# A graph attention layer with a bit-decoding MLP on one core: spins ahead of the last two tiles' features, edges prepared on Pool, x tiles loaded behind operand 6, and the MLP's second bias as a hidden unit

## The chip, the core and the metric

The kernel runs on one core of a Trainium2 chip. The metric is the device time of one execution in microseconds (us). The engines are TensorE (PE in the profile), VectorE (DVE), ScalarE (ACT), GpSimd (POOL) and SyncE (SP). SP, Pool and, where told to, ScalarE issue DMA transfers, each from a queue of its own.

## What is computed

There are N = 1250 nodes with 512 features, 20000 edges sorted by destination, and H = 4 heads of 512 columns. `_layernorm` has no scale. Cut to what matters:

```
xn    = layernorm(x)
q,k,v = xn @ Wq + bq, xn @ Wk + bk, xn @ Wv + bv          # each (n, 4, 512)
alpha = sum(q[dst] * k[src]) / sqrt(512);  attn = softmax of alpha over the edges of one dst
agg   = segment_sum(attn * v[src], dst)                    # (n, 4 * 512)
xa    = agg + xn @ Wskip + bskip
x     = x + gamma * layernorm(xa @ Wlin + blin + xa[:, :512]) + beta
z     = layernorm(x)
# three MLPs (and, or, xor): only inputs 0, 1, 44, 45, 46 can be nonzero and only output 64 is used
nibbles = argmax(z[:, 16:32] > .5), ... (four of them);  flags = z[:, 1:4]
sel   = the chosen MLP's  relu(feat @ w1 + b1) @ w2[:, 64] + b2[64], for rows 0 and 1
out   = z with 2 * one_hot(clip(round(sel), 0, 15)) added at columns 80:96 and 96:112 where active
x     = x + out
```

## The kernel before, in words

**Splits.** Each fp32 matrix is split into a high and a low part (fp32r), and a product is three matmuls of 512 columns (`mm3`, L1533 to L1535): high by high, high by low, low by high.

**Weight products.** Per head, the weights are multiplied first: G = Wq by Wk, M = Wv by Wlin, K = Wskip by Wlin, numbered p = 0 to 11. A job ("P", p, i) is the row block i (of KC = 4) of product p. Operand n (`opnd[n % 4]`) is the n-th weight in the order Wq, Wk, Wv, Wlin, Wskip of each head. SP loads it into `stage[n % 2]`, except operands 2 and 3 (Wv and Wlin of head 0), which go to `early[0]` and `early[1]`; ScalarE writes its high part (`split_hi`, L771; for the early ones `split_hi_halves`, L833, in two column halves), VectorE its low part (`split_lo`, L1012; `split_lo_halves`, L1020). Before Wlin of head 0 is split, VectorE adds the identity to its diagonal. A finished block goes from PSUM to `prod_parts` in two parts, high by ScalarE (L808) and low by VectorE (L1075), and Pool's queue stores it to HBM (`store_product`, L624). `prod_parts` has room for one product, so the high part of block i of the next product waits on `prod_out[i]`, the landing of that store.

**Edges.** In between, TensorE counts edges: for each tile of 128 destination nodes it multiplies one-hot rows of the edges' destinations and sources (`count_part`, L1652, bf16, 105 columns), by quarters of the edge tiles, behind jobs of products 1 to 10. VectorE builds the one-hot rows (`onehots`, L1034 and L1043) one job ahead. For this `edge_places` (L1079) turns the edge numbers into places and weights; it runs on VectorE at p = 0, i = 2.

**x.** Ten tiles of 128 rows. Tiles 0 to 3 go to `x_aside`, tiles 4 to 9 to `acc`. VectorE measures them (`x_moments`) at p = 2 and 3, at the jobs in MEASURED; x_moments(0) waits for all three loads. They are normalized and transposed between later jobs.

**Heads.** Each of four heads runs ten destination tiles d: scores (L1533 to L1535 into ps_s), mask, exp, weighing by counts, a transposition through HBM (`regroup` on SP's queue), and `outputs`, 10 x 3 matmuls of 512 columns. The first three heads are a loop, the last one is written out (`last_head`).

**The end.** In the last head each finished tile goes through add_out (L1347), ScalarE's squares (L908, L915), `centre` (L1377), `residual` (L1384), Pool's inverse spread (`inverse_spread`, L660 and L662), the features (VectorE L1393 to L1407, Pool's `choice` L684 to L688 and `choose` L1417), a transposition (`turn_features`, L1781), a copy by ScalarE (L929), two hidden matmuls (`hidden`, L1791, 3 x 160 columns), two dot products with w2 on VectorE (`dots`, L1431) and `results`. The second bias is chosen on Pool (`chosen_bias`, L693 and L694) and added in `results`. All but columns 80 to 112 of tiles 8 and 9 is stored ahead (`store_rest`); these columns (`store_result`, L568) follow, tile 9 from VectorE first, then tile 8 from Pool, both on SP's queue. At the program's start TensorE runs 18 matmuls on `ones` (`spin`, L1661), which nothing reads.

Of the kernel before, what the change touches and what calls it, by code (L numbers as in the profile page):

```python
# [33 lines left out]
N = 1250  # L34
# [29 lines left out]
HID = 160  # L64
SPINS = 18
BY_POOL = NT - 2
# [97 lines left out]
def graph_layer(nc, x, src, dst, weights, bias_cols, blin, gamma, beta, mlp_w1, mlp_w2, mlp_b2, out):  # L164
# [3 lines left out]
    with ExitStack() as ctx:  # L168
# [130 lines left out]
        b2_bc = put("b2_bc", [P, OPS], F32)  # L299
# [30 lines left out]
        s_b2 = [small[0:R, 80 + i:81 + i] for i in range(2)]  # L330
        s_act, s_flag = [small[0:R, 82:83], flag_pool[0:R, 0:1]], [small[0:R, 83:86], flag_pool[0:R, 1:4]]
        s_part = small[0:R, 86:89]
# [3 lines left out]
        x_in, edges_in, bias_in, tail_in = sem("x_in"), sem("edges_in"), sem("bias_in"), sem("tail_in")  # L336
        blin_in = sem("blin_in")
# [81 lines left out]

        def half_cols(i):  # L420

            return slice(D // 2 * i, D // 2 * i + D // 2)
# [63 lines left out]
        def _(sp):  # L486
# [60 lines left out]
            sp.dma_start(b2_bc[0:R, :], mlp_b2.partition_broadcast(R)).then_inc(tail_in, 16)  # L547
# [12 lines left out]

            def store_result(t):
                rows = min(R, N - R * t)
                some = slice(LO_HI_OUT, LO_HI_OUT + 32)
                if t == BY_POOL:
                    sp.wait_ge(o_pool, 1)
                else:
                    sp.wait_ge(o_ready, t)
                sp.dma_start(out[R * t:R * t + rows, some], acc[0:rows, t, some]).then_inc(out_done, 16)  # L568
# [25 lines left out]
            for t in (NT - 1, NT - 2):  # L594
                store_result(t)
# [1328 lines left out]
```

## Time and profile before

| | |
|---|---|
| three runs | 1003.58, 1234.95 and 1005.67 us; median 1005.67 |
| profiled execution | 1004.65 us; span from first to last instruction 1002.5 us |
| mean granted TensorE clock | 0.993 |
| busy share of the span | PE 98%, PEld (weight load) 80%, DVE 58%, ACT 33%, POOL 11% |
| DMA | 115.84 MB, mean 116 GB/s; in the first of 40 slices 327 GB/s |
| chain that ended last | PE 94%, DVE 2%, DMA 2%, ACT 1%, issue 1% |

All times in rows count from the span's start. A matmul's record overlaps the next one's, so the distance from start to start tells its cost, and "idle before" is shown only where the engine stood. The granted clock is a share of full speed (1.00 is 2.4 GHz, 0.50 is 1.2 GHz).

### The profile page before, as it was taken

The page shows a single profiled execution, that of the slowest core. Times are in us where ns is not written, and L with a number is a line of the kernel's source. Part 1 is how long each engine was busy: PE and PEld are TensorE (multiplying, and loading weights), DVE is VectorE, ACT ScalarE, POOL GpSimd, SP SyncE. Part 2 cuts the span into 40 slices and gives each one's busy share as a digit, 9 for nine tenths or more (in the row PEclk, how much of TensorE's full clock was granted, in tenths as well). Part 3 has the DMA queues.
Part 4 walks back from the last instruction along what each step waited for, and adds up shares of the span by engine and source line. Part 5 has one row for each costly group of instructions (what it writes and reads, how often), then busy time and mean ns, then how long its engine had stood idle before and what let it go on. Part 6 is the DMA issues. An engine that isn't in the chain of part 4 may idle for free.

```text
span 1002.5 us, 13135 instructions
## 1 busy us (share of the span) xinstructions
PE 984.4 (98%) x4841; PEld 804.8 (80%) x4841; DVE 579.2 (58%) x1225; ACT 335.0 (33%) x531; POOL 107.7 (11%) x232
## 2 busy tenths in 40 slices
PE   9999999999999999999999999999999999999994
PEld 6667777688888888888888888888888888888883
DVE  6899996452445446226454542354464325788786
ACT  4446554102233223114222321233232213435342
POOL 2121101000000000000000000000000000345465
PEclk9999999999999999999999999999999999999997
DMA  9856554400152344005323420161334103443421
GB/s 327 286 210 210 218 192 189 168 2 1 53 189 68 91 122 146 28 1 157 111 79 105 159 83 1 27 215 53 105 80 163 52 1 83 154 121 105 143 83 40
DMA packets 43561, 115.84 MB, mean 116 GB/s; under 512 B 5472, under 2 KB 26044, under 8 KB 40172
## 3 DMA queue, kind: packets, MB, share of 16 engines
q1 hardware_dynamic: 38892, 98.21, 31.5%
q0 software_dynamic: 4608, 16.78, 4.3%
q8 instruction: 43, 0.70, 0.3%
q14 instruction: 18, 0.15, 0.0%
HBM read 70.07 MB, written 44.90 MB: 115 GB/s over the span
## 4 chain that ended last, share of the span: by engine, by line
PE 94%; DVE 2%; DMA 2%; ACT 1%; issue 1%; SPq 0%; DVEq 0%
PE ps_o L1533 10%; PE ps_o L1534 9%; PE ps_o L1535 9%; PE ps_s L1534 9%; PE ps_r L1533 9%; PE ps_s L1535 9%; PE ps_s L1533 9%; PE ps_r L1535 9%; PE ps_r L1534 9%; PE ps_t L1533 2%; PE ps_t L1535 2%; PE ps_t L1534 2%; DMA stage<-in_Wk 1%; PE ps_s L1612 1%; PE ps_s L1652 1%; DMA early<-in_Wlin 1%
## 5 line engine op out<-in xcount | busy, mean ns | idle before, releaser
L1534 PE MATMUL ps_s<-xT_lo,tT 128*128 128x512 f32 (+1 forms) x480 | 168.7, 351 | 0.0
L1535 PE MATMUL ps_s<-xT_hi,tT 128*128 128x512 f32 (+1 forms) x480 | 168.4, 351 | 0.0
L1533 PE MATMUL ps_s<-xT_hi,tT 128*128 128x512 f32 (+1 forms) x480 | 168.1, 350 | 0.0
L1533 PE MATMUL ps_o<-y,pT 128*128 128x512 f32 x380 | 148.6, 391 | 0.0
L1534 PE MATMUL ps_o<-y,pT 128*128 128x512 f32 x380 | 148.0, 389 | 0.0
L1535 PE MATMUL ps_o<-y,pT 128*128 128x512 f32 x380 | 148.0, 389 | 0.0
L897 ACT ACTIVATE prob<-prob,nbias 128x1250 f32<-128x1250 f32 x40 | 53.7, 1342 | 269.5 <-DVE nbias L1296 269.5
L1290 DVE CUSTOM_DVE_ANT_0 prob<-ps_s,maskb 128x1250 f32<-128x1250 f32 x40 | 58.2, 1456 | 128.9 <-issue 128.9
L1534 PEld LDWEIGHTS ps_s<-xT_lo,tT 128*128 128x128 f32 x480 | 90.7, 189 | 14.1
L1533 PEld LDWEIGHTS ps_s<-xT_hi,tT 128*128 128x128 f32 x480 | 90.5, 189 | 14.0
L1535 PEld LDWEIGHTS ps_s<-xT_hi,tT 128*128 128x128 f32 x480 | 90.8, 189 | 12.5
L880 ACT ACTIVATE pT<-whole 128x640 fp32r<-128x640 f32 x78 | 57.1, 737 | 103.3 <-PE ps_o L1535 97.8
L1303 DVE CUSTOM_DVE_ANT_0 prob<-prob,count 128x1250 f32<-128x1250 f32 x40 | 58.4, 1459 | 46.5 <-ACT prob L897 46.5
L1535 PEld LDWEIGHTS ps_o<-y,pT 128*128 128x128 f32 x380 | 71.3, 188 | 14.9
L1533 PEld LDWEIGHTS ps_o<-y,pT 128*128 128x128 f32 x380 | 71.5, 188 | 14.4
L1534 PEld LDWEIGHTS ps_o<-y,pT 128*128 128x128 f32 x380 | 71.4, 188 | 13.7
L651 POOL MEMSET row_mask<- 108x1 f32 x1 | 0.1, 99 | 688.3 <-DMA w_raw<-in_mlp_w 688.3
L1347 DVE SCALAR_TENSOR_TENSOR acc<-ps_o,zinv,acc 128x512 f32<-128x512 f32 x38 | 28.4, 748 | 78.9 <-PE ps_o L1535 78.0
L1533 PE MATMUL ps_r<-xT_hi,gbuf 128*128 128x512 f32 (+1 forms) x192 | 67.4, 351 | 0.0
L1534 PE MATMUL ps_r<-xT_lo,gbuf 128*128 128x512 f32 (+1 forms) x192 | 67.4, 351 | 0.0
L1535 PE MATMUL ps_r<-xT_hi,gbuf 128*128 128x512 f32 (+1 forms) x192 | 67.4, 351 | 0.0
L1270 DVE TENSOR_TENSOR y<-ps_r,y 128x512 fp32r<-128x512 f32 x40 | 27.4, 684 | 66.4 <-ACT y L867 66.4
(293 smaller groups left out, 1763.0 us busy)
## 6 DMA issues: line engine op xcount, KB each, us to landing
regrouped<-prob SPq DMA_DIRECT2D x156, 160.0 KB, 2.8
whole<-regrouped SPq DMA_DIRECT2D x39, 640.0 KB, 3.9
products<-prod_parts POOLq DMA_DIRECT2D x32, 512.0 KB, 3.9
gbuf<-products SPq DMA_DIRECT2D x4, 2048.0 KB, 8.2
mbuf<-products SPq DMA_DIRECT2D x4, 2048.0 KB, 9.0
stage<-in_Wskip SPq DMA_DIRECT2D x4, 1024.0 KB, 6.0
stage<-in_Wq SPq DMA_DIRECT2D x3, 1024.0 KB, 5.5
stage<-in_Wk SPq DMA_DIRECT2D x3, 1024.0 KB, 5.9
```

The costliest lines, as they stand in the source:

```text
L651: link(nc.gpsimd.memset(row_mask[:, 0:1], 1.0))
L880: nc.scalar.activation(pT[:, 0, a:b, :].rearrange("p k (q b) -> p k q b", q=Q), whole[:, :, a:b, :].rearrange("p q k b -> p k q b"), ACT.C ...
L897: nc.scalar.activation(at_prob, at_prob, ACT.Exp, scale=SCALE, bias=nbias[0:R, d:d + 1]).then_inc(exp_done, 1)
L1270: nc.vector.tensor_tensor(y[:, 1, a, :], ps_r[:, local % 2, :], y[:, 0, a, :].bitcast(F32), ALU.subtract).then_inc(rot_free, 1)
L1290: nc.vector.tensor_tensor_reduce(at_prob, ps_s[0:R, 0:N], maskb[0:R, :], 1.0, -0.1 * MASKED, ALU.subtract, ALU.max, top[0:R, d:d + 1]).the ...
L1303: nc.vector.tensor_tensor_reduce(at_prob, at_prob, count[0:R, d, 0:N], 1.0, 0.0, ALU.mult, ALU.add, zsum[0:R, d:d + 1]).then_inc(prob_read ...
L1347: nc.vector.scalar_tensor_tensor(out=acc[0:R, d, :], in0=out_bank(d, last)[0:R, :], scalar=zinv[0:R, d:d + 1], in1=acc[0:R, d, :], op0=ALU ...
L1533: nc.tensor.matmul(out_, a[0], b[0], start=start, stop=False)
L1534: nc.tensor.matmul(out_, a[0], b[1], start=False, stop=False)
L1535: return nc.tensor.matmul(out_, a[1], b[0], start=False, stop=stop)
L1612: ins = nc.tensor.matmul(ps_uv[:, a, :], bpad[:, 1 - a, at:at + 2 * H], w[s][:, k, :], start=(h == 0 and k == 0 and s == 0), stop=(h == H ...
L1652: nc.tensor.matmul(ps_s[0:R, 0:NP], onehot_dst[t % RING][0:ER, a:a + R], onehot_src[slot][0:ER, j, 0:NP], start=(t == window(d)[0]), stop= ...
```

## The change

It has five parts.

1. HID grows from 160 to 162. The new hidden unit 160 has weight 1 at the constant feature, so its value is 1 for the chosen MLP, and its entry in w2 is b2[64]; unit 161 is zero. The load of b2, Pool's `chosen_bias` and its operand in `results` go.
2. `edge_places` moves from VectorE to Pool, ahead of all product stores; the last step is two instructions there. VectorE waits for `edges_ready` where the work stood. The four edge loads move ahead of Wv's. VectorE's half split (2, 0) moves ahead of the first product's saves.
3. The loads of x tiles 4 to 8 and of tile 9 move behind the load of operand 6. The wait for three blocks' stores ahead of them goes. x_moments(0) waits for tiles 0 to 3 only, x_moments(4) for the others.
4. In the last head the low columns of tile 8 (L1393) become a step of their own, `low_columns`, and the residual of tile 9 comes between them and the rest of tile 8's features. Tile 8's result is stored from ScalarE's queue.
5. TensorE runs 40 spins on the identity (read as bf16, 256 columns each) ahead of tile 8's feature transposition, and 8 ahead of tile 9's.

```diff
-HID = 160
+HID = 162
+LAST_SPINS = (40, 8)
...
-            for n in (3, 2):
-                sp.dma_start(early[n - 2][:], weights[n][0]).then_inc(early_in[n - 2], 16)
+            sp.dma_start(early[1][:], weights[3][0]).then_inc(early_in[1], 16)
             for i, ends in enumerate((src, dst)):
                 for a, w in EDGE_ROWS:
                     sp.dma_start(edge_i[a:a + w, i, :], ends[a:a + w, :]).then_inc(edges_in, 16)
+            sp.dma_start(early[0][:], weights[2][0]).then_inc(early_in[0], 16)
...
-            for i in range(KC - 1):
-                sp.wait_ge(prod_out[i], 16)
-            sp.dma_start(acc[:, X_ASIDE:NT - 1, :], x_tiles[:, X_ASIDE:NT - 1, :]).then_inc(x_in, 16)
-            sp.wait_ge(pads_ready, 1)
-            sp.dma_start(acc[0:LAST_ROWS, NT - 1, :], x[full:N, :]).then_inc(x_in, 16)
             for n in load_order():
                 sp.wait_ge(split_ready[n % 2], n // 2 - 1)
                 sp.dma_start(stage[n % 2][:], weights[n % 5][n // 5]).then_inc(stage_in[n % 2], 16)
+                if n == 6:
+                    sp.dma_start(acc[:, X_ASIDE:NT - 1, :], x_tiles[:, X_ASIDE:NT - 1, :]).then_inc(x_more_in, 16)
+                    sp.wait_ge(pads_ready, 1)
+                    sp.dma_start(acc[0:LAST_ROWS, NT - 1, :], x[full:N, :]).then_inc(x_more_in, 16)
...
-            for t in (NT - 1, NT - 2):
-                store_result(t)
+            sp.wait_ge(o_ready, NT - 1)
+            sp.dma_start(out[full:N, result_cols], acc[0:LAST_ROWS, NT - 1, result_cols]).then_inc(out_done, 16)
...
+            def edge_places():
+
+                pool.wait_ge(edges_in, 32 * len(EDGE_ROWS))
+                link(nc.gpsimd.tensor_copy(edge_f[0:ER], edge_i[0:ER]))
+                source, place = edge_f[0:ER, 0, :], at_plane[0:ER, :]
+                link(nc.gpsimd.tensor_scalar(place, source, -float(NP // 2), 1.0 / NP, ALU.add, ALU.mult))
+                link(nc.gpsimd.tensor_scalar(place, place, ROUND, None, ALU.add))
+                link(nc.gpsimd.tensor_scalar(place, place, ROUND, None, ALU.subtract))
+                nc.gpsimd.tensor_scalar(weight_i[0:ER, :], place, DIGIT * 2.0 ** 23, ONE_BITS, ALU.mult, ALU.add)
+                link(nc.gpsimd.tensor_scalar(place, place, -float(NP), None, ALU.mult))
+                nc.gpsimd.tensor_tensor(edge_place[0:ER, :], place, source, ALU.add).then_inc(edges_ready, 1)
+
+            edge_places()
             for p in range(3 * H):
...
-                link(nc.gpsimd.tensor_scalar(sel_, sel_, s_b2[t % 2], 0.0, ALU.add, ALU.max))
-                link(nc.gpsimd.tensor_scalar(sel_, sel_, 15.0, ROUND, ALU.min, ALU.add))
+                link(nc.gpsimd.tensor_scalar(sel_, sel_, 0.0, 15.0, ALU.max, ALU.min))
+                link(nc.gpsimd.tensor_scalar(sel_, sel_, ROUND, None, ALU.add))
...
             choice(NT - 2)
-            chosen_bias(NT - 2)
             z_factors(NT - 1)
             choice(NT - 1)
-            chosen_gate(NT - 2)
+            gates(NT - 2)
             gates(NT - 1)
             results(NT - 2)
...
                 feat_copy(NT - 1)
+                act.wait_ge(o_pool, 1)
+                act.dma_start(out[R * BY_POOL:R * BY_POOL + R, result_cols],
+                              acc[0:R, BY_POOL, result_cols]).then_inc(out_done, 16)
...
-            split_lo_halves(3)
+            split_lo_half(3, 0)
+            split_lo_half(3, 1)
+            split_lo_half(2, 0)
             for job in JOBS:
...
                 if p == 0:
                     if i == 0:
-                        split_lo_halves(2)
+                        split_lo_half(2, 1)
                     if i == 2:
-                        edge_places()
+                        dve.wait_ge(edges_ready, 1)
...
                 centre(NT - 1)
+                low_columns(NT - 2)
+                residual(NT - 1)
                 features(NT - 2)
-                residual(NT - 1)
                 choose(NT - 2)
...
-            def spin():
-
-                some = ones[:].bitcast(BF16)
-                pe.wait_ge(pool_step, 1)
-                for _ in range(SPINS):
+            def spin(some, times):
+
+                for _ in range(times):
                     nc.tensor.matmul(ps_s[:, 0:2 * P], some[:, 0:P], some, start=True, stop=True)
...
-                for t in range(NT - 2, NT):
+                for t, times in ((NT - 2, LAST_SPINS[0]), (NT - 1, LAST_SPINS[1])):
+                    spin(ident[:].bitcast(BF16), times)
                     turn_features(t)
                     hidden(t)
```

## Rows read from the trace of the kernel before

**Rows 1.** Windows: stretch, length, busy of each engine, clock, DMA share, GB/s.
```profile
110.00:985.00 875.00, 875.00 (x4293) 727.34 (x4291) 471.56 (x955) 273.99 (x413) 76.41 (x159) 1.00 0.32 100
985.00:1002.50 17.50, 4.84 (x14) 2.50 (x12) 10.37 (x41) 3.90 (x11) 10.44 (x35) 0.63 0.13 41
```

**Rows 2.** Timeline of TensorE: start, duration, instruction, idle before and its releaser.
```profile
32.40 0.41 PE L1652 MATMUL ps_s<-onehot_src,onehot_dst 125*128 125x105 bf16 x5
34.55 1.25 PE L1652 MATMUL ps_s<-onehot_src,onehot_dst 125*128 125x105 bf16 x5 [1.74 <-DVE onehot_dst L1043]
...
50.74 0.99 PE L1652 MATMUL ps_s<-onehot_src,onehot_dst 125*128 125x105 bf16 x4 [0.95 <-DVE onehot_dst L1043]
...
79.89 1.05 PE L1652 MATMUL ps_s<-onehot_src,onehot_dst 125*128 125x105 bf16 x6
```

**Rows 3.** Timeline of VectorE in the start.
```profile
15.25 2.36 DVE L1020 TENSOR_TENSOR opnd_lo<-early,opnd_hi 128x1024 fp32r<-128x1024 f32 x2
18.77 0.69 DVE L1075 TENSOR_TENSOR prod_parts<-ps_t,prod_parts 128x512 fp32r<-128x512 f32 x1 [1.16 <-ACT prod_parts L808]
...
22.84 0.32 DVE L1083 CAST edge_f<-edge_i 125x320 f32<-125x320 int32 x1
...
24.68 0.60 DVE L1034 TENSOR_TENSOR onehot_src<-node_id,edge_place 125x420 bf16<-125x420 f16 x1
...
28.41 0.68 DVE L1075 TENSOR_TENSOR prod_parts<-ps_t,prod_parts 128x512 fp32r<-128x512 f32 x1
...
34.16 1.37 DVE L1043 TENSOR_SCALAR onehot_dst<-node_id,edge_f,edge_p 125x256 bf16<-125x256 f16 x5
...
47.03 2.29 DVE L1012 TENSOR_TENSOR opnd_lo<-stage,opnd_hi 128x2048 fp32r<-128x2048 f32 x1 [2.80 <-ACT opnd_hi L771]
```

**Rows 4.** Timeline of ScalarE in the start.
```profile
26.03 0.60 ACT L808 ACTIVATE prod_parts<-ps_t 128x512 fp32r<-128x512 f32 x1 [5.90 <-DMA products<-prod_parts]
...
45.09 1.92 ACT L771 ACTIVATE opnd_hi<-stage 128x2048 fp32r<-128x2048 f32 x1 [5.79 <-DMA stage<-in_Wk]
```

**Rows 5.** Timeline of SP's queue: the issue of operand 6.
```profile
33.65 0.34 SPq L509 DMA_DIRECT2D stage<-in_Wk  x1
```

**Rows 6.** Timelines of Pool and VectorE; last, a group of Pool's by form.
```profile
19.77 0.92 POOL L624 DMA_DIRECT2D products<-prod_parts  x1 [15.56 <-DVE prod_parts L1075]
...
73.74 2.27 DVE L1012 TENSOR_TENSOR opnd_lo<-stage,opnd_hi 128x2048 fp32r<-128x2048 f32 x1
...
74.59 1.99 POOL L638 TENSOR_TENSOR nmr<-mv,rstd 128x10 f32<-128x10 f32 x1
76.67 0.34 POOL L639 TENSOR_SCALAR nmr<-nmr 128x10 f32<-128x10 f32 x1
...
L730 POOL TENSOR_TENSOR xres<-xres,beta_bc 128x512 f32<-128x512 f32 x9 | 11.7, 1295 | 0.9 <-DMA xres<-in_x 0.9
```

**Rows 7.** Timeline of the end, all engines.
```profile
988.77 0.95 POOL L662 TENSOR_TENSOR rstd<-veps,eps_pow 128x1 f32<-128x1 f32 x1
989.33 0.32 DVE L1393 TENSOR_SCALAR z_low<-acc,mv,rstd 128x80 f32<-128x80 f32 x1
...
990.75 0.76 DVE L1384 SCALAR_TENSOR_TENSOR acc<-centred,rstd,xres_last 128x512 f32<-128x512 f32 x1
...
995.26 0.66 DVE L1431 SCALAR_TENSOR_TENSOR ps_t<-ps_t,w_bc 128x480 f32<-128x480 f32 x1
...
996.29 1.14 PE L1791 MATMUL ps_t<-w_parts,featT 108*128 108x480 f32 x2 [0.41 <-ACT featT L929]
...
999.70 0.74 SPq L568 DMA_DIRECT2D out<-acc  x2
```

**Rows 8.** Windows of the end, columns as in rows 1.
```profile
985.00:990.00 5.00, 1.70 (x8) 1.08 (x6) 3.52 (x13) 1.18 (x5) 2.67 (x7) 0.94 0.14 52
...
989.00:989.50 0.50, 0.00 (x0) 0.00 (x0) 0.46 (x2) 0.00 (x0) 0.50 (x1) 0.93 0.00 0
```

**Rows 9.** The spins at the start: ns min/median/max, first and last start.
```profile
L1661 PE MATMUL ps_s<-ones x18: 394/421/421, 2.3 to 5.9; 128*128 128x256 bf16 x18
```

More of the change, by code:

```diff
@@ L329, in graph_layer @@
         s_gate = [small[0:R, 78 + i:79 + i] for i in range(2)]
-        s_b2 = [small[0:R, 80 + i:81 + i] for i in range(2)]
         s_act, s_flag = [small[0:R, 82:83], flag_pool[0:R, 0:1]], [small[0:R, 83:86], flag_pool[0:R, 1:4]]
-        s_part = small[0:R, 86:89]
         s_sel, hot = [small[0:R, 90 + 2 * i:92 + 2 * i] for i in range(2)], small[0:R, 96:128]
-        x_in, edges_in, bias_in, tail_in = sem("x_in"), sem("edges_in"), sem("bias_in"), sem("tail_in")
-        blin_in = sem("blin_in")
+        x_in, edges_in, edges_ready, bias_in, tail_in = sem("x_in"), sem("edges_in"), sem("edges_ready"), sem("bias_in"), sem("tail_in")
+        blin_in, x_more_in = sem("blin_in"), sem("x_more_in")
         g_in, m_in, xres_in, out_done = sem("g_in"), sem("m_in"), [sem(f"xres_in{i}") for i in range(3)], sem("out_done")
@@ L559, in store_rest @@
                     sp.dma_start(out[R * t:R * t + rows, a:b], acc[0:rows, t, a:b]).then_inc(out_done, 16)
[L561 to L568, printed above, removed]
             def store(t):
@@ L1013, in split_lo, with split_lo_half @@
                                                 ALU.subtract).then_inc(split_ready[odd], 1)
-            def split_lo_halves(n):
-                for half, high in enumerate((half_hi[n - 2], hi_ready[n % 2])):
-                    some = half_cols(half)
-                    dve.wait_ge(high, 1)
-                    ins = nc.vector.tensor_tensor(opnd[n][1][:, :, some], raw(n)[:, :, some],
-                                                  opnd[n][0][:, :, some].bitcast(F32), ALU.subtract)
-                    if half:
-                        ins.then_inc(split_ready[n % 2], 1)
-                    elif n == 2:
-                        ins.then_inc(half_split, 1)
+            def split_lo_half(n, half):
+                some = half_cols(half)
+                dve.wait_ge(hi_ready[n % 2] if half else half_hi[n - 2], 1)
+                ins = nc.vector.tensor_tensor(opnd[n][1][:, :, some], raw(n)[:, :, some],
+                                              opnd[n][0][:, :, some].bitcast(F32), ALU.subtract)
+                if half:
+                    ins.then_inc(split_ready[n % 2], 1)
+                elif n == 2:
+                    ins.then_inc(half_split, 1)
             def onehots(b):
@@ L1386, in residual, with low_columns @@
                                                accum_out=stats[0:R, t, 2:3]).then_inc(res_ready, 1)
-            def features(t):
+            def low_columns(t):
                 z = z_low[t % 2]
@@ L1394, in features @@
                                         ALU.subtract, ALU.mult).then_inc(z_low_ready, 1)
+            def features(t):
+                z = z_low[t % 2]
                 dve.wait_ge(z_low_ready, t + 1)
@@ L1439, in results @@
                 dve.wait_ge(gate_ready, t + 1)
-                chain(nc.vector.tensor_scalar(sel_, sel_, s_b2[t % 2], 0.0, ALU.add, ALU.max))
-                chain(nc.vector.tensor_scalar(sel_, sel_, 15.0, ROUND, ALU.min, ALU.add))
+                chain(nc.vector.tensor_scalar(sel_, sel_, 0.0, 15.0, ALU.max, ALU.min))
+                chain(nc.vector.tensor_scalar(sel_, sel_, ROUND, None, ALU.add))
                 for r in range(2):
@@ L1654, in count_part @@
                                      stop=(t == window(d)[-1])).then_inc(onehot_used, 1)
-            def spin():
-                some = ones[:].bitcast(BF16)
-                pe.wait_ge(pool_step, 1)
-                for _ in range(SPINS):
+            def spin(some, times):
+                for _ in range(times):
                     nc.tensor.matmul(ps_s[:, 0:2 * P], some[:, 0:P], some, start=True, stop=True)
-            spin()
+            pe.wait_ge(pool_step, 1)
+            spin(ones[:].bitcast(BF16), SPINS)
             first_product()
@@ L1894 @@
         for r in range(2):
[L1895 to L1897 removed]
+            feats[:, o, r:4:2, r, o, 0:HID - 2] = np.stack([w1[o][i] for i in (0, 1)])
+            feats[:, o, 4 + 3 * r:7 + 3 * r, r, o, 0:HID - 2] = np.stack([w1[o][i] for i in (46, 44, 45)])
+            feats[:, o, 10 + r, r, o, 0:HID - 2] = b1[o]
+            feats[:, o, 10 + r, r, o, HID - 2] = 1.0
     arrays = {
```

43 lines of the change are left out of this document (12 added, 31 removed).

## The prediction, made before the change was run

> **What bounds the kernel now.** I read the windows by stretch first: from 110 to 985 us TensorE's busy time equals the stretch, and the last 17.5 us hold only 4.84 us of it, at a mean granted clock of 0.63 [rows 1]. No edit shortens TensorE's work in the full stretch, so time is won or lost in two places: the start, up to about 100 us, and the end, after the last wide matmul. Busy times of matmuls overlap, so in the start I went by TensorE's timeline and looked for small matmuls with a releaser or a stretched duration. There are three stalls, each in the matmuls that count edges [rows 2]. The first, at 34.55: idle 1.74 us, and then five matmuls take 1.25 us where five took 0.41 just before; 1.74 + 0.84 = 2.6 us. The second, at 50.74: idle 0.95 us, and four take 0.99 instead of 0.41 x 4/5 = 0.33; 1.6 us. The third, at 79.89: six take 1.05 instead of 0.49; 0.6 us. The releaser of the first two is VectorE's one-hot rows (L1043), so VectorE's timeline comes next, then what VectorE waited for.
>
> **The start, first stall.** VectorE works without a gap from 22.84 us to 34.16 + 1.37 = 35.5 us, the end of the one-hots that TensorE waits for. First in it stands the edge preparation, from 22.84 to 24.68: 1.84 us, which moves to Pool [rows 3]. The half split of operand 2 that moves ahead of the first product's save also fills the 1.16 us in which VectorE waited before 18.77 [rows 3]. So the first one-hots could start up to 1.84 + 1.16 = 3.0 us earlier, less some 0.6 us, my guess for Wv landing behind four edge transfers: 22.3 us, if Pool is done. That gain isn't passed on whole. ScalarE starts the high part of product (1,0) at 26.03 us, when the store of product (0,0) has landed, and takes 0.60 [rows 4]; so VectorE's save of (1,0), at 28.41 before [rows 3], can't start ahead of 26.7. From that save to the one-hots' end are 35.5 - 28.4 = 7.1 us of gapless work, which gives 33.8: a gain of 1.7, or 1.9 if the store lands a little earlier.
>
> That store stands on Pool's queue, issued at 19.77 us [rows 6], and the edge work is now ahead of it there. The edges follow Wlin, which has landed when VectorE splits it at 15.25 [rows 3]; say 14 us. The trace has no Pool row of 125x160: below it lies 128x10 with one input, 0.34 us, above it 128x512 with two, 1.29 us [rows 6]. That is 0.34 and 1.9 ns an element, so at most 0.64 for 160 columns and 0.95 for the copy of 320. Eight instructions: 2.7 to 5.4 us; I take 4, in the middle as the shapes are, done near 18 us if nothing holds Pool.
>
> Something can hold it. A Pool instruction of 128x10 with two inputs took 1.99 us, begun at 74.59 while VectorE ran a split of two SBUF inputs from 73.74 to 76.01, and ended after that split [rows 6]. The splits of operands 3 and 2 run from 15.25 on, 1.18 us a half [rows 3], just where Pool's edge chain falls.
> The Trainium skill, SBUF — State Buffer, section "Who interferes with whom", says that a VectorE instruction with two SBUF inputs contends with a GpSimd instruction that reads SBUF, and that whichever issues second blocks fully. The row of 1.99 us agrees. By that rule the forecast of a free Pool is too good; the held case below is what it would make of this kernel.
> Priced from rows, if four half splits hold one Pool instruction each for about 1 us, the chain ends near 22. The store leaves 2 us or so later than 19.77; it took 6.3 us before, behind loads that will have drained further, so I let it land near 27. VectorE then reaches the end of the one-hots at 27.0 + 0.6 + 7.1 = 34.7, a gain of 0.8. Between 1.7 (free) and 0.8 (held), with ends 1.9 and 0, I take **1.1**.
>
> **The start, second stall.** VectorE sat idle 2.80 us ahead of the split of operand 6 at 47.03 [rows 3], since ScalarE waited 5.79 us for Wk until 45.09 [rows 4]. Wk was issued at 33.65 [rows 5], behind the x tiles, and took 11.4 us to land. Now the x tiles go behind it. Issued at about 32.7, Wk needs to be in place when ScalarE is through with its saves and VectorE with its own work, 2.8 + 1.1 us ahead of 45.09: by 41.2, after 8.5 us. The store of the same congested start took 6.3 with half the bytes [rows 4, 6], so this isn't sure. If it is in time, VectorE gains 1.1 + 2.8 = 3.9 us by this point and TensorE needs 1.1 + 1.6 = 2.7, a margin of 1.2: the whole **1.6** goes (1.0 if Wk lands 1.8 us late, 0 if it lands no earlier). Load 7 leaves SP some 0.9 us later than it would (two x issues); its split comes seven microseconds behind operand 6's, which covers it, as it covers x itself, whose tiles from 4 on are first read there. The wait for the zeroed pad rows, now on SP ahead of load 7, is over since the program's start.
>
> **Later stalls.** VectorE comes out 1.2 us further ahead of TensorE than before, and the third stall of 0.6 can go, with another like it near 96; from 0 to 1.1, I take **0.5**. The start gives 1.1 + 1.6 + 0.5 = **3.2**, ends 0 and 4.6.
>
> **The end.** Of the window from 985 to 990 us TensorE fills the first 1.70, so its last wide matmul ends at 986.7, and the clock goes to 0.50 only in the last tenth of a microsecond ahead of 989.5 (0.93 over that half microsecond) [rows 8]. Then VectorE, ScalarE and Pool pass the last tile's statistics around. VectorE writes the low columns of tile 8 at 989.33, goes through its features until 990.75 and only then runs the residual of tile 9 [rows 7]. Now the residual comes right behind the low columns, once Pool's spread is ready: 988.77 + 0.95 = 989.72, or 989.8. That is 0.95 us earlier, and what hangs on it (square, spread, features and choice of tile 9) moves along up to the dot products of tile 8, from 995.26 to 994.3 [rows 7]. The features of tile 8 are 0.25 later, about 992, which still leaves 2.3 us for their transposition, copy and hidden matmuls.
> VectorE then has four dot products of 0.66 us: 994.3 + 2.65 = 997.0. Before, the last two waited for tile 9's hidden matmuls, begun at 996.29, a pair of which took 1.14 us at clock 0.50 [rows 7, 8]; the first was done at about 997.05, and two dot products later it was 998.4. So the gain is 1.4 if the hidden matmuls are in time, and 0.95 if the clock stays at half.
> The spins: 18 of 256 columns at the start lie (5.9 - 2.3)/17 = 0.21 us apart [rows 9]; at full clock eight matmuls of 512 columns pass in 1.70 us [rows 8], 0.21 each, so 256 take 0.11. Forty behind 986.7 take 4.3 us, until 991.0, a microsecond ahead of the transposition; eight behind tile 8's hidden matmuls take 0.9, until about 994, ahead of tile 9 as well. They delay nothing then. The bias leaves Pool's chain, off the path, and six columns more in a dot product (486 for 480) add 0.66/80 = 0.01 us. Both results end near 998.2, and their stores, 0.74 us for two issues in a row on one queue [rows 7], leave from two: 0.37 more. ScalarE's queue is used for the first time, which no row prices; -0.6 to +0.2 around it. The end gives 1.4 + 0.4 = **1.8**, ends 0.7 and 2.2.
>
> **Sum.** The profiled execution took 1004.65 us, 2.15 beside its span, and lies 1.0 under the median of 1005.67. 1004.65 - 3.2 - 1.8 = **999.7 us**.
>
> **Rivals.** (1) The splits hold Pool's chain so long that the first stall and the later ones stay: 1004.65 - 1.6 - 1.8 = 1001.3. For it: the 1.99 us row; against: only four splits, with saves between them. (2) Wk still lands late, since the product stores share the transfers: 1004.65 - 1.6 - 1.8 = 1001.3 too, by the first stall and the later ones alone. (3) The clock falls under the spins near 989.4: twenty-four are through, sixteen at 0.21 end near 992.8, the eight follow late hidden matmuls by 1.7 us, and tile 9's transposition comes some 1.4 us later than before. With 0.4 won by the stores: 1004.65 - 3.2 + 1.0 = 1002.5. Against it: the clock stood through 2.7 us without any matmul. (4) The other side: Pool gets no turn until VectorE itself stops for it near 22.8, and needs 3.5 us more. The store leaves at 26.3 and with the old 6.3 us lands at 32.6; VectorE's save starts at 33.2, 4.8 us behind before, and TensorE with it. Against it stand the second stall and the end, 3.4: 1004.65 + 4.8 - 3.4 = 1006.1. It decides from a landing at 31.2 on (28.4 - 0.6 + 3.4).
>
> **Chances.** Forecast, with its own range 998 to 1001: 0.55. Rival 1: 0.17, rival 2: 0.13, rival 3: 0.09, rival 4: 0.06. The range goes from 997.0, nearly the high ends of both sums (4.6 and 2.2 give 997.9) and 0.9 of scatter, to 1004.0, rivals 1 to 3 and 1.5 of scatter; it leaves rival 4 out. A measurement tells about 2%, 20 us, from no change. No case reaches that either way, as all the idle time of start and end sums to less: 0.02 faster, 0.96 within, 0.02 slower for what I haven't seen.
>
> **What would show it.** First stall: VectorE's first one-hots before 23.5 us and under 1.9 us lost near 33; Pool instructions of over 1 us in the edge chain would show the hold. Second: ScalarE's high part of operand 6 begun by 41 us. The end: a residual of tile 9 some 3.1 us behind the last wide matmul, not 4.05; a clock of 1.00 up to the last hidden matmul; and transpositions that don't follow right on a spin. The prediction fails if the store of product (0,0) lands past 28 us, if the spins run at 0.21, or if the shifts in the start meet a wait for a transfer that was hidden before.

## The result, and the profile after

The changed kernel takes 998.47 us (median of six runs, 998.14 to 1000.15) where the kernel before takes 1004.23 (six runs, median). The ratio is 0.9947, with an interval from 0.9933 to 0.9961: 5.3 us faster, between 3.9 and 6.7, which is within 2%. The ratio compares fast executions alone and leaves out one of the kernel before, which took 1234.95 us. The profiled execution took 998.3 us, its span 996.4. The forecast was 999.7 and the range 997.0 to 1004.0.

I divide each execution at the end of the last wide matmul of the last tile (L1522 to L1524), which is 982.24 us here and was 986.70 before. What lies behind it, the end part, takes 996.4 - 982.24 = 14.16 us; before it took 15.8. So the two profiled executions differ by 4.46 us in the start and by 1.64 in the end part.

**The start.** TensorE's timeline has the same groups of counting matmuls as [rows 2]:

```profile
30.20 0.41 PE L1641 MATMUL ps_s<-onehot_src,onehot_dst 125*128 125x105 bf16 x5
33.27 0.98 PE L1641 MATMUL ps_s<-onehot_src,onehot_dst 125*128 125x105 bf16 x10
...
47.96 0.46 PE L1641 MATMUL ps_s<-onehot_src,onehot_dst 125*128 125x105 bf16 x6
```

TensorE waits ahead of none of them. The ten at 33.27 are the two groups that stood at 32.40 and 34.55 before; they take 0.98 us for 0.82, so 0.2 is left of the first stall's 2.6. At 47.96 stand six in one group; before they were two, a wait, and the four at 50.74. VectorE's timeline answers to [rows 3]:

```profile
16.32 3.75 DVE L1013 TENSOR_TENSOR opnd_lo<-early,opnd_hi 128x1024 fp32r<-128x1024 f32 x3
...
22.92 0.58 DVE L1027 TENSOR_TENSOR onehot_src<-node_id,edge_place 125x420 bf16<-125x420 f16 x1
...
26.86 0.69 DVE L1068 TENSOR_TENSOR prod_parts<-ps_t,prod_parts 128x512 fp32r<-128x512 f32 x1
...
32.61 1.36 DVE L1036 TENSOR_SCALAR onehot_dst<-node_id,edge_f,edge_p 125x256 bf16<-125x256 f16 x5
```

The three half splits run without a gap, the first one-hots start 1.76 us earlier than before, and the save of block (1,0), at 26.86 for 28.41, starts as soon as it can. From there to the end of the one-hots, 33.97, are 7.1 us, as forecast. ScalarE's timeline answers to [rows 4]:

```profile
26.15 0.60 ACT L799 ACTIVATE prod_parts<-ps_t 128x512 fp32r<-128x512 f32 x1 [5.01 <-DMA products<-prod_parts]
...
37.91 1.92 ACT L762 ACTIVATE opnd_hi<-stage 128x2048 fp32r<-128x2048 f32 x1 [0.18 <-DMA stage<-in_Wk]
```

The store of product (0,0) landed at 26.15, and operand 6 was there 7.2 us earlier than before. Pool's timeline is new here:

```profile
15.18 0.45 POOL L633 CAST edge_f<-edge_i 125x320 f32<-125x320 int32 x1 [10.97 <-DMA edge_i<-in_dst]
15.72 0.34 POOL L635 TENSOR_SCALAR edge_i<-edge_f 125x160 f32<-125x160 f32 x1
16.15 0.64 POOL L636 TENSOR_SCALAR edge_i<-edge_i 125x160 f32<-125x160 f32 x1
16.88 1.16 POOL L637 TENSOR_SCALAR edge_i<-edge_i 125x160 f32<-125x160 f32 x1
18.12 0.87 POOL L638 TENSOR_SCALAR edge_p<-edge_i 125x160 int32<-125x160 f32 x1
19.06 1.49 POOL L639 TENSOR_SCALAR edge_i<-edge_i 125x160 f32<-125x160 f32 x1
20.63 1.56 POOL L640 TENSOR_TENSOR edge_place<-edge_i,edge_f 125x160 f16<-125x160 f32 x1
22.14 2.38 POOL L613 DMA_DIRECT2D products<-prod_parts  x3
```

One form, 125x160 with one input, takes 0.34 us before VectorE's splits begin and up to 1.49 beside them (four of them, between 16.32 and 21.80): the hold of the prediction. In run e9 (below), whose chain comes later, the last instruction (L640) takes 0.52 us, as no split is left then, and not 1.56:

```profile
22.58 0.52 POOL L640 TENSOR_TENSOR edge_place<-edge_i,edge_f 125x160 f16<-125x160 f32 x1
```

The chain of seven takes 7.0 us, and the store leaves at 22.14, with two others behind it.

Two things more stand in TensorE's timelines. The later stalls are gone: before, the groups at 76.63, 79.89 [rows 2] and 96.31 took 0.2, 0.6 and 0.5 us more than an undisturbed one, 1.3 altogether, and after none does. And the first weight product starts 1.04 us later than before (7.05 us for 6.01), of which 0.87 is left at 33.27; in the other traces of kernels with this start it begins between 5.83 and 6.73, so this is scatter and no gain or loss of the change. The first line is of the kernel before, the others are of the changed one:

```profile
96.31 0.99 PE L1652 MATMUL ps_s<-onehot_src,onehot_dst 125*128 125x105 bf16 x6
...
7.05 0.73 PE L1564 MATMUL ps_t<-opnd_hi 128*128 128x512 f32 x2 [0.69 <-ACT opnd_hi L819]
...
76.30 0.47 PE L1641 MATMUL ps_s<-onehot_src,onehot_dst 125*128 125x105 bf16 x6
...
92.04 0.46 PE L1641 MATMUL ps_s<-onehot_src,onehot_dst 125*128 125x105 bf16 x6
```

**The end.** The windows of the end, columns as in [rows 1], and its timeline, which answers to [rows 7]:

```profile
982.24:987.00 4.76, 4.38 (x40) 3.69 (x38) 3.43 (x12) 2.62 (x7) 2.44 (x8) 1.00 0.15 57
987.00:992.00 5.00, 3.11 (x14) 1.63 (x14) 3.88 (x17) 1.37 (x4) 4.22 (x17) 1.00 0.27 85
992.00:996.40 4.40, 0.00 (x0) 0.00 (x0) 1.59 (x7) 0.00 (x0) 1.29 (x4) 0.67 0.04 7
```

```profile
985.30 0.75 DVE L1367 SCALAR_TENSOR_TENSOR acc<-centred,rstd,xres_last 128x512 f32<-128x512 f32 x1
...
987.00 0.19 POOL L662 TENSOR_SCALAR veps<-stats 128x1 f32<-128x1 f32 x1 [0.20 <-ACT junk L906]
...
989.83 0.66 DVE L1419 SCALAR_TENSOR_TENSOR ps_t<-ps_t,w_bc 128x486 f32<-128x486 f32 x1
...
990.72 1.00 PE L1779 MATMUL ps_t<-w_parts,featT 108*128 108x486 f32 x2 [0.41 <-ACT featT L920]
...
993.23 0.25 POOL L713 TENSOR_TENSOR acc<-acc,hot_pool 128x32 f32<-128x32 f32 x1
993.51 0.38 ACTq L984 DMA_DIRECT2D out<-acc  x1
993.54 0.19 DVE L1436 TENSOR_TENSOR acc<-acc,ones 128x32 f32<-128x32 f32 x1
993.76 0.32 SPq L584 DMA_DIRECT2D out<-acc  x1
```

The residual of tile 9 comes 3.06 us behind the last wide matmul and the first dot product 7.59; before it was 4.05 and 8.56. The granted clock is 1.00 as far as 992, behind the last hidden matmul; only then does it fall to its lower level (1.2 GHz). The second of the two result stores is issued at 993.76. What follows stands in no timeline, but in the view by source line, where the end of the program has line 169 (168 before), that of the block around it. Each engine's sequencer has a drain there, and SP's branch stands behind its wait for all stores:

```profile
L169 POOLq EVENT_SEMAPHORE  x2: 17/17/17, 996.2 to 996.3; - x2
...
L169 POOLq DRAIN  x1: 3005/3005/3005, 993.2 to 993.2; - x1
...
L169 SPq COMPARE_BRANCH  x1: 38/38/38, 995.1 to 995.1; - x1
L169 SPq DRAIN  x1: 7/7/7, 995.3 to 995.3; - x1
```

These columns are duration in ns (min, median, max) and first and last start in us. So SP is through at 995.1. Pool's drain starts with Pool's last instruction, takes 3.0 us, and ends at 996.2, 2.7 us behind that instruction's end; then the program ends. The kernel before has the same pair:

```profile
L168 POOLq DRAIN  x1: 3062/3062/3062, 999.2 to 999.2; - x1
...
L168 SPq COMPARE_BRANCH  x1: 38/38/38, 1001.5 to 1001.5; - x1
```

The expectations of the experiments were written without these rows, and argue with dot products and stores.

### The profile page after: what moved, and what is told of

It reads as the page before. It is cut to its first block, busy times and chain, and to the rows that moved or that the text cites. A ratio compares the mean times of both kernels' runs of the same rounds, so it can differ in the third digit from the quotient of the medians.

```text
span 996.4 us, 13209 instructions
## 1 busy us (share of the span) xinstructions
PE 986.7 (99%) x4889; PEld 807.9 (81%) x4889; DVE 576.6 (58%) x1219; ACT 335.9 (34%) x531; POOL 108.8 (11%) x219
## 4 chain that ended last, share of the span: by engine, by line
PE 99%; DMA 1%; DVE 0%; issue 0%; ACT 0%; SPq 0%
PE ps_o L1522 10%; PE ps_o L1523 10%; PE ps_o L1524 10%; PE ps_r L1522 9%; PE ps_r L1524 9%; PE ps_r L1523 9%; PE ps_s L1523 9%; PE ps_s L1524 9%; PE ps_s L1522 9%; PE ps_t L1522 3%; PE ps_t L1524 2%; PE ps_t L1523 2%; PE ps_s L1601 1%; PE ps_s L1641 1%; PE ps_t L1564 1%; PE ps_s L1648 1%
## 5 line engine op out<-in xcount | busy, mean ns | idle before, releaser
L1524 PE MATMUL ps_s<-xT_hi,tT 128*128 128x512 f32 (+1 forms) x480 | 168.4, 351 | 0.0
L1522 PE MATMUL ps_s<-xT_hi,tT 128*128 128x512 f32 (+1 forms) x480 | 168.1, 350 | 0.0
L1522 PE MATMUL ps_o<-y,pT 128*128 128x512 f32 x380 | 148.6, 391 | 0.0
L1524 PE MATMUL ps_o<-y,pT 128*128 128x512 f32 x380 | 148.0, 389 | 0.0
L1522 PEld LDWEIGHTS ps_s<-xT_hi,tT 128*128 128x128 f32 x480 | 90.6, 189 | 14.2 <-issue 0.2
L1524 PEld LDWEIGHTS ps_s<-xT_hi,tT 128*128 128x128 f32 x480 | 90.7, 189 | 12.5
L1524 PEld LDWEIGHTS ps_o<-y,pT 128*128 128x128 f32 x380 | 71.3, 188 | 14.9
L1522 PEld LDWEIGHTS ps_o<-y,pT 128*128 128x128 f32 x380 | 71.4, 188 | 14.4
L1522 PE MATMUL ps_r<-xT_hi,gbuf 128*128 128x512 f32 (+1 forms) x192 | 67.4, 351 | 0.0
L1524 PE MATMUL ps_r<-xT_hi,gbuf 128*128 128x512 f32 (+1 forms) x192 | 67.4, 351 | 0.0
```

Of the source, the lines that this page charges most:

```text
L1522: nc.tensor.matmul(out_, a[0], b[0], start=start, stop=False)
L1524: return nc.tensor.matmul(out_, a[1], b[0], start=False, stop=stop)
```

## The experiments on the start

A ratio is a run's time over that of the kernel before in the same batch, with its 95% interval. The end part is the span less the end of the last wide matmul, in the profiled execution. All ratios below lie within 2% of 1.

**Run e5_before_again**: the kernel before once more, unchanged.

> The kernel before, unchanged, for the scatter of its start. Two kernels with the same start (the spins alone, the residual first) ended their last wide matmul at 983.9 and 984.3 us, not 986.7. Theory A (Wk's landing behind the x tiles varies between executions, and with it the second stall): the end of the last wide matmul lies between 983.5 and 987, and where it is early, ScalarE's wait for Wk ends near 42 and not 45 us. Theory B (the edits at the end moved the start by their code): it is at 986.7 again, within 0.3. The stretch behind it stays at 15.8 us under both.

One run: 1002.74 us. The last wide matmul ends at 984.91, 1.8 us earlier than in the profile of before. ScalarE's wait for Wk ends at 42.95, not 45.09, and there is no second stall; the first is there:

```profile
34.94 1.24 PE L1652 MATMUL ps_s<-onehot_src,onehot_dst 125*128 125x105 bf16 x5 [1.40 <-DVE onehot_dst L1043]
```

Two experiments below have the start of the kernel before as well: their last wide matmuls end at 984.28 (e3) and 983.91 (e4), and neither has the second stall. So the start scatters by 2.8 us between executions, and the 1.6 of the second stall was a draw of the profiled one: three of the four traces with this start lack it. The first stall scatters too: 2.6, 2.2 (e5), 1.8 (e3) and 1.6 us (e4).

**Run e1_edges_alone**: the kernel before with part 2 of the change only.

```diff
-            for n in (3, 2):
-                sp.dma_start(early[n - 2][:], weights[n][0]).then_inc(early_in[n - 2], 16)
+            sp.dma_start(early[1][:], weights[3][0]).then_inc(early_in[1], 16)
...
+            sp.dma_start(early[0][:], weights[2][0]).then_inc(early_in[0], 16)
...
-            split_lo_halves(3)
+            split_lo_half(3, 0)
+            split_lo_half(3, 1)
+            split_lo_half(2, 0)
...
-                        edge_places()
+                        dve.wait_ge(edges_ready, 1)
```

> The kernel before with the edges' preparation on Pool, their loads ahead of Wv's and the moved half split, nothing else. Theory A (the parts of the start depend on each other): the first stall of 2.6 us nearly goes, but Wk is still queued behind the x tiles, so VectorE's split of operand 6 stays near 47 us while TensorE comes 2.4 us earlier, and the second stall grows from 1.6 to 3 or 4 us. The last wide matmul ends 0 to 1 us ahead of 986.7; the time falls by 0 to 1 us. Theory B (each stall is worth its own length): the second stall stays at 1.6, the time falls by 2.4 us. Theory C (Pool, held by VectorE's splits, gives the stall back): the first one-hots start after 24 us, the store of product (0,0) lands past 28, no gain and a first stall of over 2 us.

Ratio 0.9999 (0.9988 to 1.0011), median 1003.38 beside 1003.82. TensorE's timeline:

```profile
33.36 1.07 PE L1652 MATMUL ps_s<-onehot_src,onehot_dst 125*128 125x105 bf16 x10
...
50.10 1.04 PE L1652 MATMUL ps_s<-onehot_src,onehot_dst 125*128 125x105 bf16 x4 [1.68 <-DVE onehot_dst L1055]
```

The first stall is gone, but 1.68 + 0.71 = 2.4 us are lost at the second place, where VectorE's work hangs on Wk, for which ScalarE waited until 44.45. Alone, this part only brings TensorE earlier to the next wait.

**Run e2_x_behind_operand6**: the kernel before with part 3 only.

```diff
-            for i in range(KC - 1):
-                sp.wait_ge(prod_out[i], 16)
-            sp.dma_start(acc[:, X_ASIDE:NT - 1, :], x_tiles[:, X_ASIDE:NT - 1, :]).then_inc(x_in, 16)
...
+                if n == 6:
+                    sp.dma_start(acc[:, X_ASIDE:NT - 1, :], x_tiles[:, X_ASIDE:NT - 1, :]).then_inc(x_more_in, 16)
...
```

> The kernel before with only the x tiles' loads moved behind operand 6. Theory A: VectorE's idle 2.8 us before the split of operand 6 goes, the second stall of 1.6 with it, and the later ones of 0.6 and 0.5 too; the first stays at 2.6. The last wide matmul ends 1.6 to 2.7 us earlier, the time falls by as much. Rival (the load was late for other transfers' sake, the product stores): ScalarE still waits for Wk past 43 us, the second stall stays above 1 us, and the time falls by under 1 us.

Ratio 0.9989 (0.998 to 0.9999), median 1002.43. Wk is in place at 39.58, where ScalarE waits 0.23 us for it. The first stall stays:

```profile
34.63 1.25 PE L1653 MATMUL ps_s<-onehot_src,onehot_dst 125*128 125x105 bf16 x5 [1.55 <-DVE onehot_dst L1042]
```

**Run e8_start_edits_both**: the diffs of e1 and e2 together on the kernel before, with its old end.

> The kernel before with both edits of the start (edges on Pool, x behind operand 6) and the old end. Theory A (they depend on each other): the first and second stalls both go, the last wide matmul ends at 982 to 982.5, 2 to 4 us earlier than before's executions, more than the sum of the two alone (0 and 1.1 us by the times). Theory B (they add): 1.1 us. The end stays at 15.8.

Ratio 0.9967 (0.9956 to 0.9979), median 1000.67: 3.3 us, where the parts gave 0.1 and 1.1. The last wide matmul ends at 982.19, as in the changed kernel, and the end part takes 15.8, as before. So most of the gain of the start belongs to the pair: two waits in a row on one path. Without the first alone TensorE stops at the second (e1); without the second alone it still stops at the first (e2). By the times this is only just clear of the noise: the two parts together reach up to 3.2 us at the ends of their intervals, and the pair lies between 2.1 and 4.4. The stalls in the three traces carry it.

**Run e9_edges_behind_wv**: the changed kernel with the edge loads behind Wv, as they were before.

```diff
             sp.dma_start(early[1][:], weights[3][0]).then_inc(early_in[1], 16)
+            sp.dma_start(early[0][:], weights[2][0]).then_inc(early_in[0], 16)
             for i, ends in enumerate((src, dst)):
                 for a, w in EDGE_ROWS:
                     sp.dma_start(edge_i[a:a + w, i, :], ends[a:a + w, :]).then_inc(edges_in, 16)
-            sp.dma_start(early[0][:], weights[2][0]).then_inc(early_in[0], 16)
```

> The changed kernel with the four edge loads behind Wv again, as before the change. In the five traces so far with the edge loads ahead of Wv, VectorE gets Wlin at 13.9 to 14.5 us, in the five without at 12.8 to 13.6. Theory A (that is lost on no path: TensorE's second product starts near 21.6 in both): the edges land some 2 us later, Pool's chain ends near 24 instead of 22, the store of product (0,0) lands at 27 to 28, and the time is 0.5 to 1.5 us longer. Theory B (the early landing of Wlin is worth its 0.9 us): the time falls by up to 0.9 us.

Ratio 0.9965 (0.9952 to 0.9978), median 998.86; run e10, in the same batch, has 0.995 and 998.72. The edges land 2.0 us later, at 17.21, and Pool ends its chain at 23.1. VectorE waits for it:

```profile
23.14 0.60 DVE L1027 TENSOR_TENSOR onehot_src<-node_id,edge_place 125x420 bf16<-125x420 f16 x1 [1.01 <-POOL edge_place L640]
```

TensorE's ten matmuls at 32.96 take 1.57 us, 0.6 more than after; but in e10, with the order of the change, they take 1.70. So the order of the loads is worth between 0.1 us (medians) and 1.5 (ratios), too little to tell.

**Run e11_edge_chain_longer**: the changed kernel with four Pool instructions more in the edge chain, which multiply by one.

```diff
+                for _ in range(4):
+                    link(nc.gpsimd.tensor_scalar(place, place, 1.0, None, ALU.mult))
```

> The changed kernel with four more instructions of 125x160 (times 1.0) in Pool's edge chain. The chain took 7.0 us. Theory A (Pool stands on the path through the store of product (0,0), as rival 4 had it): the chain ends 2.5 to 4 us later, near 25 to 26, VectorE waits for it from 22.9 on, the store lands at 28 to 30 and the first stall grows by 2 to 4 us, the time as much. Theory B (the store's landing is set by the transfers ahead of it, and VectorE has room): it still lands by 27, and the time grows by under 1.5 us.

Ratio 0.9977 (0.9967 to 0.9986), median 1001.2: 2.5 us slower than e10 in the same batch. The four take 4.59 us beside the splits, the chain ends at 23.87, and VectorE waits for it:

```profile
23.90 0.60 DVE L1029 TENSOR_TENSOR onehot_src<-node_id,edge_place 125x420 bf16<-125x420 f16 x1 [1.99 <-POOL edge_place L642]
```

The store of product (0,0) lands at 27.17, a microsecond later than after, and the first stall is back with 1.42 + 0.84 us at 34.02. VectorE's one-hots end at 34.99, a microsecond later than after. So Pool's chain stands on the path; after, it ended 0.7 us ahead of VectorE's use (22.2 to 22.92), but the store followed it at once. There is a second loss, in the windows, columns as in [rows 1]:

```profile
36.00:40.00 4.00, 4.00 (x12) 2.62 (x11) 4.00 (x12) 1.76 (x2) 1.26 (x2) 0.57 0.98 322
```

Behind the stall the clock falls to its lower level for nearly these four microseconds, and wide matmuls start every 0.43 us, not every 0.23. Run e7 has the same, by chance:

```profile
36.00:40.00 4.00, 4.00 (x12) 3.07 (x11) 4.00 (x13) 1.87 (x2) 1.38 (x2) 0.57 0.98 357
```

There the store landed at 27.68. From the stalled matmuls to the next group are 7.4 us (34.53 to 41.93); in e12, whose stall at 34.46 was 0.3 us shorter and whose clock stayed, 5.8. So a first stall can cost 1.6 us more than its own length, and 1.6 of the 2.2 us by which the last wide matmul ends later in e11 than after are of this kind. The stall of the kernel before [rows 2] was longer and left the clock at 1.00; what decides stays open. The two slowest executions of e9 (1001.84 and 1001.56 us, at a mean clock of 0.997 and 0.996, where the other five have 0.998 or 0.999 and at most 999.72) may be of this kind; they have no profile.

## The experiments on the end

**Run e3_residual_first**: the kernel before with part 4 without the other queue.

```diff
                 centre(NT - 1)
-                features(NT - 2)
+                low_columns(NT - 2)
                 residual(NT - 1)
+                features(NT - 2)
```

> The kernel before with only the end's order changed: residual of tile 9 between the low columns of tile 8 and the rest of its features. Theory A: residual of tile 9 starts 3.1 us behind the last wide matmul instead of 4.05, everything behind it is 0.95 us earlier, the clock is at half in the last hidden matmuls, and the time falls by 0.9 to 1.0 us. Rival (Pool's spread is what the residual waits for): it starts as late as before, and nothing is won.

Ratio 0.9999 (0.9989 to 1.0008), and an end part of 15.42, only 0.38 shorter, which the times can't show. The residual starts at 3.05 us behind the last wide matmul, as wanted, but Pool isn't free when its square is there. Its timeline:

```profile
988.90 0.20 POOL L693 TENSOR_TENSOR ones<-ones,b_bc 128x3 f32<-128x3 f32 x1
989.21 0.39 POOL L694 TENSOR_SCALAR ones<-ones 128x1 f32<-128x1 f32 x1
989.66 0.19 POOL L660 TENSOR_SCALAR veps<-stats 128x1 f32<-128x1 f32 x1
```

The choice of tile 8's bias (L693, L694) stands ahead of tile 9's spread. In the changed kernel the spread starts at 987.00 - 982.24 = 4.76; here at 989.66 - 984.28 = 5.38.

**Run e4_spins_alone**: the kernel before with part 5 only.

```diff
+LAST_SPINS = (40, 8)
...
-                for t in range(NT - 2, NT):
+                for t, times in ((NT - 2, LAST_SPINS[0]), (NT - 1, LAST_SPINS[1])):
+                    spin(ident[:].bitcast(BF16), times)
```

> The kernel before with only the 40 and 8 spins. Theory A: they are 0.11 us apart and end before tile 8's features are there, the clock stays at 1.00, and the first hidden matmul of tile 9 is done some 0.45 us earlier, which is the gain. Rival 1: VectorE's dot products of tile 8, until 996.6, are what tile 9's wait for anyway, so the gain stays below 0.5 whatever the clock does. Rival 2: spins at 0.21 us hold the transpositions, and the end is 1 us or more later.

Ratio 0.9993 (0.9983 to 1.0003), end part 15.79: nothing. The third dot product started 0.45 us earlier, at 9.92 behind the last wide matmul for 10.37, and nothing came of it.

**Run e6_bias_on_pool**: the changed kernel without part 1, so with the bias on Pool.

```diff
-HID = 162
+HID = 160
...
+                link(nc.gpsimd.tensor_tensor(s_part, s_w[t % 2], b2_bc[0:R, :], ALU.mult))
+                nc.gpsimd.tensor_scalar(s_b2[t % 2], s_part[:, 0:1], s_part[:, 1:2], s_part[:, 2:3], ALU.add, ALU.add)
...
             choice(NT - 2)
+            chosen_bias(NT - 2)
             z_factors(NT - 1)
```

> The changed kernel with the second bias back on Pool (162 columns back to 160). Theory A (with the residual early, Pool's two bias instructions of tile 8 stand ahead of the spread of tile 9): the low columns of tile 9 start 0.6 us later, 6.25 behind the last wide matmul instead of 5.63, and the end takes 14.6 to 14.8 us instead of 14.2. Theory B (the bias is off the path, as predicted): 14.2 us, no difference.

Ratio 0.9966 (0.9954 to 0.9977), median 1000.09, end part 15.38: 1.2 us more than after, where I had expected 14.6 to 14.8. Pool's last instruction starts 12.16 us behind the last wide matmul, after 10.99: the bias of tile 8 delays the spread by 0.62, and that of tile 9 takes 0.66 between its choice and its gate.

**Run e7_no_spins**: the changed kernel without its 48 spins.

```diff
-LAST_SPINS = (40, 8)
+LAST_SPINS = (0, 0)
```

> The changed kernel without the 48 spins at the end. Theory A: the clock goes to half 2.7 us behind the last wide matmul, the hidden pair of tile 9 takes 1.14 instead of 0.7 and its first half is done some 0.25 us later than tile 8's last dot product; the end is 0.2 to 0.5 us longer. Rival (VectorE is what binds, with tile 8's dot products until then): under 0.1 us. The spins were forecast at 0.45.

Ratio 0.994 (0.9923 to 0.9956), median 998.02, end part 14.18, as with spins. The clock is at 0.50 from 989 us on, and VectorE's result comes at 11.79 us behind the last wide matmul instead of 11.30; Pool's last instruction comes at 10.95 for 10.99. This execution's start was a bad draw (985.22).

**Run e10_tile8_stored_by_sp**: the changed kernel with both results stored from SP's queue, tile 8 first.

```diff
+            sp.wait_ge(o_pool, 1)
+            sp.dma_start(out[R * BY_POOL:R * BY_POOL + R, result_cols],
+                         acc[0:R, BY_POOL, result_cols]).then_inc(out_done, 16)
             sp.wait_ge(o_ready, NT - 1)
...
-                act.wait_ge(o_pool, 1)
-                act.dma_start(out[R * BY_POOL:R * BY_POOL + R, result_cols],
-                              acc[0:R, BY_POOL, result_cols]).then_inc(out_done, 16)
```

> The changed kernel with tile 8's result stored from SP's queue, ahead of tile 9's, and not from ScalarE's. In three traces the span ends 2.9 us behind ScalarE's issue, where two issues on SP's queue were followed by the end 2.4 us behind the second. Theory A (ScalarE's queue, used for the first time, takes some 0.5 us more and sets the end): the end takes 14.0 to 14.1 us instead of 14.16, so nothing was won by the second queue. Theory B (two queues save the 0.37 us of an issue, as predicted): 14.4 to 14.5 us.

Ratio 0.995 (0.9937 to 0.9963), median 998.72, end part 14.09: the second queue gives nothing. Here I read e6, e7 and e10 wrongly. In all three the span ends 2.9 us behind the issue of tile 8's store, and I took that for the time such a store needs.

**Run e12_by_sp_no_spins**: e10 and e7 together, to see whether the slow store had hidden the spins' worth.

```diff
-LAST_SPINS = (40, 8)
+LAST_SPINS = (0, 0)
...
+            sp.wait_ge(o_pool, 1)
+            sp.dma_start(out[R * BY_POOL:R * BY_POOL + R, result_cols],
+                         acc[0:R, BY_POOL, result_cols]).then_inc(out_done, 16)
```

> The changed kernel without its 48 spins and with the result of tile 8 stored from SP's queue. Theory A: without spins VectorE's result came 0.5 us later (11.79 us behind the last wide matmul for 11.30), and only ScalarE's slow store hid that; with both stores on SP's queue the last one follows VectorE's result, so the end is 14.09 + 0.5 = 14.6 us from the last wide matmul's end to the span's end, and the spins are worth 0.5 in this form. Theory B: the spins are worth nothing in any form of the end, and the end stays within 0.15 us of 14.1. Both expect a median within 1 us of that of the changed kernel, as the start is its own.

Ratio 0.9956 (0.9942 to 0.9971), median 999.47, end part 14.13. VectorE's result was late (11.79) and its store issued at 12.01, 0.4 later than in e10, yet the end didn't move: theory B. The rows say why:

```profile
L169 POOLq DRAIN  x1: 3003/3003/3003, 994.4 to 994.4; - x1
...
L169 SPq COMPARE_BRANCH  x1: 38/38/38, 996.8 to 996.8; - x1
L169 SPq DRAIN  x1: 7/7/7, 997.0 to 997.0; - x1
```

All stores had landed at 996.8, and the program ended at 997.6, with Pool's drain through at 997.4. Read so, all executions with a profile agree (us behind the last wide matmul's end; spans are rounded to 0.1 us, so the last two columns are good to 0.05):

| kernel | Pool's last instruction starts | SP through with the stores | end | end less Pool's start |
|---|---|---|---|---|
| before | 12.55 | 14.8 | 15.80 | 3.25 |
| before again (e5) | 12.52 | 14.8 | 15.79 | 3.27 |
| e3, residual first | 12.18 | 14.4 | 15.42 | 3.24 |
| e4, spins alone | 12.52 | 14.6 | 15.79 | 3.27 |
| e6, bias on Pool | 12.16 | 13.9 | 15.38 | 3.22 |
| after | 10.99 | 12.9 | 14.16 | 3.17 |
| e7, no spins | 10.95 | 13.4 | 14.18 | 3.23 |
| e10, both by SP | 10.94 | 13.1 | 14.09 | 3.15 |
| e12, both by SP, no spins | 10.96 | 13.3 | 14.13 | 3.17 |

In e1, e2, e8, e9 and e11 the last column is 3.25, 3.27, 3.28, 3.21 and 3.19. Counted from the end of Pool's last instruction (0.31 us long in the kernels of the first four rows, 0.25 in the others), the span ends 2.94 us later in all of them, the five others included. The end less SP's time varies from 0.8 to 1.4 (unrounded). In e6 Pool's last instruction comes 1.2 us later than after and the end 1.2 later; in e12 VectorE's result comes 0.5 later and the end doesn't move. So Pool's last instruction sets the end, and stores, spins and VectorE's result have room, in e12 still some 0.4 us: SP's own drain stands at 997.0, Pool's ends at 997.4. An edit that shortens the drain, or takes the last work off Pool, wasn't tried, and why the drain takes this long stays open.

The Trainium skill, VectorE: DVE Perf Modes, section "The DRAIN you can't avoid", gives the drains around a program as some 12 ns on all five engines. SP's (7 ns) and VectorE's (17 ns) are of that size here, ScalarE's (148 ns after) and TensorE's (543) are not, and Pool's is 3.0 us in every execution. The measurement decides for this kernel; whether the page means these drains, no run here shows.

## Why the prediction was right, and where its steps were not

The sum was 3.2 + 1.8; the profile shows 4.46 + 1.64, and the runs 5.3 altogether, of which e8 gives the start 3.3. The forecast lies 1.2 us above the median. The two totals are near, but not all terms are, and some errors cancel.

- **First stall, 1.1.** In the profile of after it went nearly whole (2.4 us), with the chain near the held case: done at 22.2 and the store landed at 26.15, not near 27. It took 4.0 us from issue to landing, where the forecast allowed some 5. But this was a good draw. What was left of the stall is 0.0 us in e6, 0.2 after, 0.6 in e8, 0.9 in e10, 1.8 in e12 and 2.0 in e7, and it follows the landing: 25.9, 26.15, 26.4, 27.0, 27.6 and 27.7. The mean of these six is 0.9; that of the five traces with the first stall in its old form (before, e2 to e5) is 2.1. So the gain is 1.2 on the mean, and the size was right. The condition stated for a failure, a landing past 28 us, was set too late: at 27.6 most of the gain was gone already. The chain has seven instructions and not eight, so its bounds from the rows should have been 2.4 and 4.8 us, not 2.7 and 5.4, and the middle 3.6 instead of 4.
- **Second stall, 1.6.** Its mechanism was right in the profile, but e5, e3 and e4 have no such stall. What makes Wk's early landing worth something is e1 against e8: with the first stall gone, the second place is the next wait. I had added the two as independent terms.
- **Later stalls, 0.5.** Against the profile mis-sized: all three went, 1.3 us. The profiled starts differ by 2.4 + 1.6 + 1.3, less the 0.9 by which TensorE began later: 4.4 of the 4.46. But e3, e4 and e5 have only 0.3 to 0.7 us of later stalls, nearly all of it near 94, so 0.5 was a fair size for an execution without the second stall.
- **The end, 1.4 for the dot products and 0.4 for the queues.** The sum was near (1.64), the mechanism wrong, so that it came out near is luck. The step that failed is "the bias leaves Pool's chain, off the path". Pool's chain is the path: the residual, priced at 0.95, gives 0.38 alone (e3), and the bias, priced at nothing, 1.2 on top of all others (e6). The spins, priced at the 0.45 between 1.4 and 0.95, and the second queue, priced at 0.4, are worth nothing (e4, e7, e10, e12). I followed the profile's chain of waits, which ends with VectorE's last instruction, and didn't look at what the program waits for behind it.
- **Rivals.** (1) The hold is real (0.34 against 1.49 us, and 0.52 against 1.56), but only four splits cause it, and the chain still ends 0.7 us ahead of its use. The row of 1.99 us was weaker evidence than I took it for: in all 14 traces that instruction stands beside the split, so no row has it free. (2) Wk was in time in e2 and after (0.2 us of wait). (3) The clock stayed up: forty spins passed in 4.38 us, 0.11 each, as priced. (4) Pool always got turns between the splits.

## What to carry to other kernels

Find what ends last before pricing the end of a kernel: look at the last instruction of each engine, and at each engine's drain, which stands only in the view by source line. Two waits in a row on one path are one term, not two; undo each alone before crediting either. Profile the kernel before more than once before pricing a stall that hangs on a transfer, and the changed kernel more than once before calling the stall gone.

## What was not expected of the hardware

Pool's drain at the end of the program takes 3.0 us (3003 to 3062 ns) in all 14 profiled executions, and the span ends 2.94 us behind the end of Pool's last instruction. SP is through its wait for the result stores 1.3 to 1.5 us behind the last issue (e12: 995.48 to 996.8). After a stall near 34 us the clock fell to 1.2 GHz at 36.4 and was back at 39.8 in two of the 14 executions, at a cost of 1.6 us.
